# Adding attention masks with 32x32 tiles of the TensorE array instead of a 128x128 identity

## The reference

```python
# layer 0: cross attention to ctx, causal
scores = jnp.where(causal, scores, -jnp.inf); attn = softmax(scores)
# layer 1: cross attention, no mask
# layer 2: causal self attention, then cross attention without mask, then a dense FFN,
#          then a mixture whose 8 experts are attentions of their own (no mask)
# layer 3: self attention with rope, window: token q sees keys q-64 .. q
```

## Time and profile before

| what | value |
|---|---|
| three timed runs, median (lowest to highest) | 3347.18 us (3345.81 to 3347.89) |
| span of the profiled execution | 3447.8 us |
| instructions | 64821 |
| PE busy | 2817.4 us, 82% of the span |
| DVE busy | 1989.0 us, 58% |
| ACT busy | 1326.8 us, 38% |
| POOL busy | 635.1 us, 18% |
| mean granted TensorE clock | 0.896 |

### The profile page before, as it was taken

How to read it: one execution, slowest core, us unless ns; L and a number is a source line. 1 busy time by engine, 2 the same in 40 slices (tenths; PEclk the granted TensorE clock), 3 DMA queues, 4 the chain that set the end, 5 groups by cost and what they waited for, 6 DMA issues and landing times.

```text
span 3447.8 us, 64821 instructions
## 1 busy us (share of the span) xinstructions
PE 2817.4 (82%) x24730; PEld 1996.0 (58%) x24818; DVE 1989.0 (58%) x6643; ACT 1326.8 (38%) x3062; POOL 635.1 (18%) x847
## 2 busy tenths in 40 slices
PE   5788988766687987988988988988988988987953
PEld 2344766634574864764764764755755755656743
DVE  2566444456544455666666666666766766765532
ACT  2343434433474743333333333334334334334521
POOL 0122112322312011121121121121111111111043
PEclk7888999877898998998998999998999999998977
DMA  7300647400373700000000000000000000003454
GB/s 254 113 23 22 199 129 208 131 19 22 125 229 99 240 23 7 3 9 7 3 9 7 3 9 7 3 9 7 3 9 7 3 9 4 3 4 112 130 168 147
DMA packets 146658, 217.14 MB, mean 63 GB/s; under 512 B 20392, under 2 KB 99248, under 8 KB 146224
## 3 DMA queue, kind: packets, MB, share of 16 engines
q1 hardware_dynamic: 134064, 187.80, 17.8%
q0 software_dynamic: 12288, 25.19, 2.4%
HBM read 159.83 MB, written 53.08 MB: 62 GB/s over the span
## 4 chain that ended last, share of the span: by engine, by line
PE 58%; DVE 21%; ACT 10%; issue 5%; another core or an unknown queue 2%; SPq 2%; DMA 1%; POOL 1%; DVEq 0%; POOLq 0%; ACTq 0%
PE bank L447 5%; PE bank L383 5%; ACT ex L1153 5%; PE bank L540 4%; PE bank L622 4%; DVE mx L1615 4%; PE bank L548 4%; PE bank L389 3%; PE bank L604 3%; PE bank L467 3%; PE bank L457 3%; PE bank L451 3%; PE bank L436 3%; PE bank L374 2%; PE bank L430 2%
## 5 line engine op out<-in xcount | busy, mean ns | idle before, releaser
L1153 ACT ACTIVATE ex<-bank 128x512 f32<-128x512 f32 x896 | 472.1, 600 | 692.7 <-PE bank L457 456.7
L1615 DVE TENSOR_REDUCE mx<-bank 128x4 bf16<-128x512 f32 x640 | 407.6, 684 | 133.2 <-PE bank L436 68.9
L965 POOL TENSOR_TENSOR rstd<-vare,power 128x2 f32<-128x2 f32 x192 | 136.1, 709 | 1377.9 <-DVE vare L1406 1377.9
L1032 POOL TENSOR_TENSOR oT<-oT 128x128 f32<-128x128 f32 x256 | 118.3, 462 | 916.2 <-DVE oT L1734 915.6
L540 PE MATMUL bank<-qm,expert 128*128 128x128 f32 x1872 | 260.2, 283 | 16.9 <-DMA expert<-in_moe 9.3
L974 POOL DMA_INDIRECT sent<-tail_tok,pos x192 | 192.0, 1000 | 394.0 <-DVE pos L1543 349.9
L383 PE MATMUL bank<-hT,wproj 128*128 128x256 f32 x736 | 242.8, 426 | 25.2 <-DVE oT L1734 8.5
L1607 DVE RECIPROCAL rden<-bank 128x16 f32<-128x16 f32 x160 | 41.1, 257 | 384.9 <-PE bank L476 347.1
L447 PE MATMUL bank<-qm,kf 32*128 32x512 f32 x1280 | 211.4, 723 | 57.1 <-ACT ex L1153 36.2
L540 PEld LDWEIGHTS bank<-qm,expert 128*128 128x128 f32 x1872 | 237.0, 198 | 28.6 <-DMA expert<-in_moe 15.5
L622 PEld LDWEIGHTS bank<-ev,ex 128*128 128x128 f32 x2048 | 247.6, 193 | 5.2 <-issue 0.4
(11 more groups left out here) (208 smaller groups left out, 5064.8 us busy)
## 6 DMA issues: line engine op xcount, KB each, us to landing
expert<-in_moe SPq DMA_DIRECT2D x78, 578.0 KB
expert<-in_moe SPq DMA_DIRECT2D x78, 512.0 KB
expert<-in_moe SPq DMA_DIRECT2D x78, 384.0 KB
sent<-zeros SPq DMA_DIRECT2D x8, 2560.0 KB, 12.8
ex<-sent SPq DMA_DIRECT2D x234, 64.0 KB
answered<-qm SPq DMA_DIRECT2D x234, 64.0 KB
ctxT<-ctx_kept SPq DMA_DIRECT2D x32, 128.0 KB
wproj<-in_wproj SPq DMA_DIRECT2D x1, 3072.0 KB
```

What stands on the lines that cost most here:

```text
L1153: give(nc.scalar.activation(ex[s][:, i], ps[:].rearrange("p (i q) -> p i q", i=4), ACT.Exp, scale=SCALE), *key)
L1615: give(nc.vector.tensor_reduce(mx[s][:, b, HB * i:HB * i + HB], ps[:].rearrange("p (i k) -> p i k", i=HB), AX.X, ALU.max), *k, "s", b, i)
```

## The change

A mask depends only on key minus query, so each strip of 32 rows of it is a piece of one pattern with an offset. The change stores, per mask, one pattern of 32 rows and 224 columns (`MASK_COLS`), repeated on the four groups of 32 partitions, and adds the mask to a bank by four products of 32x32 (identity 32x32, rows `r`, output partitions `32c` to `32c+31`) with 512 columns each, that read the pattern at offset `left`. Within a bank the four products take four different row groups and four different output groups; over four banks, 16 products use each 32x32 tile of the array once. Instead of 16 mask products with 128x128 weights per call of `attend` there are 64 of 32x32. The DMA of masks grows from 128x640 to 128x1024 float32, the cast from 128x512 to 128x896. Last, the costs that `choose_order` sees are lowered.

```diff
+STRIP = 32
+STRIPS = P // STRIP
+MASK_COLS = 2 * P - STRIP
-        masks = sb("masks", [P, 4, P], BF16)
+        masks = sb("masks", [P, 4, MASK_COLS], BF16)
...
+                    def add_mask(ps, which, then=None):
+                        for i, at in enumerate(ps):
+                            for c in range(STRIPS):
+                                r = band_rows((c + i) % STRIPS)
+                                left = P - STRIP - STRIP * c
+                                mm = nc.tensor.matmul(at[band_rows(c), :], identb[r, 0, r],
+                                                      masks[r, which, left:left + P].unsqueeze(1)
+                                                      .to_broadcast([STRIP, HB, P]), start=False, stop=then is not None)
+                            if then is not None:
+                                filled(mm, *then(i))
...
                         if mask is not None:
-                            for i in range(2):
-                                filled(nc.tensor.matmul(ps[i][:], identb[:, 0, :], masks[:, 2 * mask, :].unsqueeze(1)
-                                                        .to_broadcast([P, HB, P]), start=False, stop=True),
-                                       *k, "s", b, j + i)
+                            add_mask(ps, 2 * mask, lambda i: (*k, "s", b, j + i))
...
                         if mask is not None:
-                            for j in range(BANDS):
-                                nc.tensor.matmul(ps[j][:], identb[:, 0, :], masks[:, 2 * mask + 1, :].unsqueeze(1)
-                                                 .to_broadcast([P, HB, P]), start=False, stop=False)
+                            add_mask(ps, 2 * mask + 1)
...
-                    more = 0.0 if mask is None else 0.45
+                    more = 0.0 if mask is None else 0.25
...
-                    yield "unit", 2.9 + 3 * more, 0.6
+                    yield "unit", 2.9 + 2 * more, 0.6
...
-                    yield "unit", 3.0 + 2 * more, 0.8
+                    yield "unit", 3.0 + more, 0.8
...
-            sp.dma_start(masks_f32, A["masks"]).then_inc(sem["first_weights_in"], 16)
+            sp.dma_start(mask_land[:, 0:4 * MASK_COLS + P], A["masks"]).then_inc(sem["first_weights_in"], 16)
```

More of the change, by code:

```diff
@@ L310, in build @@
         n_loads = len(loads) + len(spread) + 1
-        masks_f32 = hid[0][:, 0, 0:3, :].rearrange("p a n -> p (a n)")[:, 0:5 * P].rearrange("p (m k) -> p m k", m=5)
+        mask_land = hid[0][:].rearrange("p a c n -> p (a c n)")
+        masks_f32 = mask_land[:, 0:4 * MASK_COLS].rearrange("p (m k) -> p m k", m=4)
+        earlier_f32 = mask_land[:, 4 * MASK_COLS:4 * MASK_COLS + P]
         x_dram = A["x"].rearrange("(s b) t f -> s t b f", b=HALF)
@@ L373, in turn_normed @@
                     for n in range(idle):
-                        nc.tensor.matmul(ps[:], identb[:, 0, :], masks[:], start=True, stop=True)
+                        nc.tensor.matmul(ps[:], identb[:, 0, :], masks[:, :, 0:P], start=True, stop=True)
                     pe.wait_ge(sem[f"ln_ready{s}"], w.next(f"ln_ready{s}"))
@@ L1355, in _ @@
             dve.wait_ge(sem["first_weights_in"], 16 * n_first)
-            nc.vector.tensor_copy(masks[:], masks_f32[:, 0:4, :]).then_inc(sem["consts_set"], 1)
-            nc.vector.tensor_copy(countb[:, 0, :], masks_f32[:, 4, :]).then_inc(sem["consts_set"], 1)
+            nc.vector.tensor_copy(masks[:], masks_f32).then_inc(sem["consts_set"], 1)
+            nc.vector.tensor_copy(countb[:, 0, :], earlier_f32).then_inc(sem["consts_set"], 1)
             nc.vector.tensor_copy(identb[:, 0, :], ident[:]).then_inc(sem["consts_set"], 1)
@@ L1976, in laid_out @@
     a["ident"] = one
-    q, k = np.arange(P)[:, None], np.arange(P)[None, :]
-    causal, window = k <= q, (k <= q) & (k >= q - WINDOW)
+    own_row, away = np.arange(P)[:, None] % STRIP, np.arange(MASK_COLS)[None, :] - (P - STRIP)
+    seen, turned_seen = away <= own_row, away >= own_row
+    allowed = (seen, turned_seen, seen & (away >= own_row - WINDOW), turned_seen & (away <= own_row + WINDOW))
     earlier = np.arange(P)[:, None] < np.arange(P)[None, :]
-    a["masks"] = np.stack([np.where(m, 0.0, NEG) for m in (causal, causal.T, window, window.T)] + [earlier], 1)\
-        .astype(np.float32)
+    a["masks"] = np.concatenate([np.where(m, 0.0, NEG) for m in allowed] + [earlier], 1).astype(np.float32)
     own = np.arange(P)[:, None] // D % NE == np.arange(NE)[None, :]
```

## The result

The changed kernel takes 3337.39 us (median of 8 runs, 3330.71 to 3343.41), the kernel before 3349.87 us beside it (8 runs, 3345.81 to 3359.24): a ratio of 0.9958, 95% interval 0.9942 to 0.9974. It is 12.5 us faster; 26 were forecast. Side and range hold, the size is less than half.

What follows compares the result with a forecast made beforehand. PE's order of work was taken to bound the kernel, with mask products on its chain. Terms: -44 (cheaper adds) + 17 (new order) + 1 (start) = -26 us, so 3347 - 26 = 3321 us; range 3282 to 3354 us.

Steps and rivals of the forecast that it cites:

- The adds, 0.43 and 0.37 us each: Mask products per call of `attend`: four banks 0.43 us instead of 0.87, two banks 0.37 instead of 0.45 or 0.53.
- Rival C: Mask adds: no two row groups in one bank, 510 us more PE time, about 3830 us; chance 0.05.
- Rival B: Mask adds: only four tiles at a time (3386 us) or issue at the steady pace (about 3355 us); chance 0.10.
- 59 x 0.75 = 44 us: Stages with nearly the old order: 59 us of mask savings on the chain, a quarter lost to later waits, 44 left.
- the 12 us of the re-ordered stretch: Layer 0, 160 to 345 us: its part of the 71 us saved on masks, taken out because the order is new.
- the clock may fall oftener with less work on PE: Whole kernel: a possible loss from a lower PE clock, given no size and left in the range.
- The order, +17 us: Layer 0: both streams in step make four rounds 4.2 us longer each, 17 us lost.
- 49.5: Layer 0's in-step round in us, built from layer 1's 51.25 us round, against 45.3 in the old order.
- Rival A: Layer 0: the new order costs nothing, rounds of 45.3 us or below, 55 us gained, 3292 us; chance 0.22.
- rival D: In-step rounds of 53 us and a second quarter of the gain lost to waits: +2 us, 3349 us; chance 0.13.
- The start, +1 us: Ahead of the first product: a larger mask load and 0.3 us more cast, about 1 us on the chain.
- Layers 2 and 3: 256 to 251: Repeating stretch of layers 2 and 3: falls from 256 to about 251 us; wrong if under 3 or over 8.

Runs made afterwards that it cites:

- 3440 level: Label for sets of runs in which every kernel takes longer: the kernel before took 3433 to 3441 us in four sets, the changed kernel 3500.
- direct sends: GpSimd's 192 indirect token-scattering DMAs made direct: against 3351.2 us, changed kernel 3332.11, kernel before 3351.03, tiles in the old order 3319.08.
- 3350 level: Label for the faster sets of runs: the kernel before took 3350 us in two sets, the changed kernel 3337.

## Why the prediction was right in its side and wrong in its size

**The adds, 0.43 and 0.37 us each: right in kind, a little too dear.** 16 tiles hold the queue for 0.37 us, eight for 0.34. A call gives PE 1.6 us and not 2 x 0.44 + 4 x 0.12 = 1.4, so 77 us in all and not 65. Rival C (3.5 us) is out, and so is the rule of the Trainium skill ("TensorEngine Tiling (Array Packing)", Restrictions and Gotchas) on different row tiles in one bank, for this use: four row groups wrote to one bank within 0.37 us, where one after another takes 0.88. Rival B (0.8 us) is out as well. (Its second price, about 3355 us, does not follow from its terms: 2 x (0.81 - 0.87) + 4 x (0.54 - 0.49) is 0.08 us more a call, 4 us in all, and with the 17 to 22 us of the order about 3370.)

**"59 x 0.75 = 44 us": the step that failed.** In the old order the tiles gave 32 us where the forecast's own working, with the 12 us of the re-ordered stretch, would have given (59 + 12) x 0.75 - 1 = 52. The quarter that I took off was for later waits, and waits did take 16 of 77 us, 21%. But 33 us more, 43%, went where I had put no term: to other instructions of PE that then ran at half speed. The prediction had it as a remark, "the clock may fall oftener with less work on PE", and left it to the range; it was the largest deduction. That the clock accounts for the 33 us is worked out from busy time and clock (33 against 34 us). Three things support it: the unchanged products have the same shortest and longest lengths in both kernels and a larger mean, one and the same kernel at two clocks differs by 40 us of busy time where the working gives 46, and PE work added or taken away moved the clock up or down. No run held the clock and changed nothing else, and the runs with work added or taken away were all at the 3440 level.

**The order, +17 us: about the right size, put together wrongly.** The changed order costs 13 us in the runs with direct sends (3332.1 against 3319.1): 16.6 us in layer 0 and 1.5 in the middle, less 6.3 in the last stretch, which I had counted as nothing. In layers 2 and 3 the query projection is the one step of PE's list that the order moved; no run moved it alone. The in-step rounds are 46.2 us in the mean, not 49.5, against 44.4 in the old order with tiles: 4 x 1.8 = 7 us. Most of the rest is lost before, while the streams come into step: these rounds begin at 170.2 us in the changed kernel and at 161.4 in the other. 49.5 was too long because layer 1's 51.25 us held the stalls. With 46.7 us from the changed kernel's trace my own steps give 46.7 - 2.5 - 1.0 + 0.4 + 0.9 + 0.5 = 45.0. The clock in the re-ordered stretch is 0.82, below 0.86 as forecast, but that was luck: in the old order with tiles it is 0.80. Rival A (free) is out, and so are the rounds of 53 us of rival D, at this level. D's other half, a second quarter of the gain lost, is about what came (29.5 x 37 / 44 = 25 us outside layer 0 by D, 25.7 in the table), though to the clock and not to waits. At the 3440 level D's order is what happened, and worse: +35.5 us.

**The start, +1 us:** the first weighing stands 1.6 us later in both kernels with tiles.

**Layers 2 and 3: 256 to 251.** From the wrong base, and the fall came out near the forecast by luck: 498.4 / 2 = 249.2 us before at the 3350 level, 491.6 / 2 = 245.8 with the change, 3.4 us less where 5 were expected and under 3 would have been wrong. In the old order the same stretch has 247.45 us: the tiles alone gave 1.8 us, less than the 3 below which I had called the forecast wrong, and the other 1.6 are the order's, which I had put at nothing.

**The base.** "3% of 26 is under 1 us" took the profiled execution for a stretched copy of the timed ones. It was not stretched but held stalls in places, some of them in layer 1. The sign that I passed over stood in the numbers shown: a span 100.6 us over three runs that agreed within 2.1 us. The L467 row with 11.9 us of idle time put down to `issue` was the trace of it.

The sum, for the changed kernel with direct sends at the 3350 level, from the table: layer 0 with the start +9.5 (forecast: 17 + 1 less about 7, so 11), the middle stretch -1.3, the rest -24.4 (forecast for both 44 - 7 = 37 gained, measured 25.7). The miss of this sum is in the term of 44. Together -16.2, as the spans (3346.6 and 3330.4). With its own sends the changed kernel gave 12.5.

**What stays open.** What makes the 3440 level: it was there in the first set and not in the one with direct sends at 3350 us, both on the chip of the same number. Why tiles in the old order lose 24 us there: they stall more (L480: 29.1 us of `issue`, against 11.9 for L467), but why a denser stretch meets the sends so much worse is not shown. Nor is what holds the engines in a stall, since `issue` and `remote` name nothing that the profile shows. The kernel before was not run with direct sends at that level. So it is not known either whether the tiles would win there without the stalls. The tiles with direct sends take 3364.9 us there against 3319.1 at the 3350 level, so 46 us are not the sends. Of the 53 us between their two profiled executions 40 stand in PE's busy time, at the lower clock, but why the clock is lower there is open. The 3319.1 us, the best time of all, belong to a kernel that doesn't place its tokens; the tiles in the old order with their true sends came up at the 3440 level only (1.0066 to 1.0079). That they would reach about 0.991 at the other is what the worthlessness of direct sends there suggests, not a measurement.

## What to carry to other kernels

Products that use a corner of the array can be packed 16 at a time in its 32x32 tiles, in one bank too. But work taken off a nearly full PE does not count in full, even where the chain runs through it: work out the time at the lower clock from the mean, 2 x (1 - clock) x span, before and after, and in a case like this one expect a good part of the saving to return as slower neighbours. When the profiled execution lies far outside the timed runs, look in it for single instructions with `issue` or `remote` ahead of them before building a term on any of its rounds. And an order of steps whose costs were fitted to old durations is a change of its own, to be run separately.

## What the hardware showed that I had not expected

- Sixteen products of 32x32 weights and 512 columns hold PE for 0.37 us, with one for each tile of the array; 0.22 us of it is one stream. Eight hold it for 0.34.
- GpSimd's indirect DMAs can slow PE, ACT and DVE at once: 98 us of 3463 in one set of runs (tiles in the old order), nothing in another (the kernel before, 3351.2 and 3351.0 us).
- The time at 1.2 GHz rose from 602 to 684 us when 77 us of PE work went, with the instructions otherwise the same. One kernel in two sets of runs had 684 and 796 us at 1.2 GHz.
